# A transformer block with a mixture of experts: head weights split in the keys' loop, experts' down weights split on GpSimd, down as six fp32r products, result stored by tiles

## The reference, cut to what matters

```python
# experts: 2048 tokens, 8 of 64 experts each, rows sorted by expert
gu = lax.ragged_dot(xs, jnp.swapaxes(gate_up_proj, 1, 2), group_sizes)   # 512 -> 2 x 192
gate, up = jnp.split(gu, 2, axis=-1)
hact = jax.nn.silu(gate) * up
y = lax.ragged_dot(hact, jnp.swapaxes(down_proj, 1, 2), group_sizes)     # 192 -> 512
out = jnp.zeros_like(x).at[tok].add(y * w[:, None])
...
# cross attention: 16 heads of 128
q = (hidden_states @ Wq).reshape(B, Sq, H, D)
k = (encoder_hidden_states @ Wk).reshape(B, Skv, H, D)
k = rmsnorm(k, gk)
...
return out @ Wo
```

## Time and profile before

| what | us |
|---|---|
| median of 3 runs (2829.97 to 2833.83) | 2832.93 |
| the profiled execution | 2839.08 |
| its span, first to last instruction | 2837.6 |
| TensorE busy | 2485.7 |
| VectorE busy | 1863.6 |
| ScalarE busy | 1280.9 |
| GpSimd busy | 1542.7 |

### The profile page before, as it was taken

How to read it: one execution, slowest core, us unless ns; L and a number is a source line. 1 busy time by engine, 2 the same in 40 slices (tenths; PEclk the granted TensorE clock), 3 DMA queues, 4 the chain that set the end, 5 groups by cost and what they waited for, 6 DMA issues and landing times. The chain is left out here.

```text
span 2837.6 us, 42365 instructions
## 1 busy us (share of the span) xinstructions
PE 2485.7 (88%) x11365; PEld 1766.0 (62%) x11366; DVE 1863.6 (66%) x3083; ACT 1280.9 (45%) x2516; POOL 1542.7 (54%) x1262
## 2 busy tenths in 40 slices
PE   6898987679793899999999937999999999999797
PEld 2333432267572677777777725778778777877553
DVE  6999999868462346654444456776775776565596
ACT  4566664343562333321222204555555555555385
POOL 2656565432555667676666545655664764444122
PEclk8999999979896899999999967999999999999899
DMA  6989898735675999987777654543444443332101
GB/s 201 289 271 296 267 295 270 218 138 197 237 271 198 334 339 315 342 287 257 265 264 247 204 170 141 180 140 125 158 138 135 159 156 112 123 115 90 60 1 60
DMA packets 271500, 572.10 MB, mean 202 GB/s; under 512 B 26993, under 2 KB 92657, under 8 KB 270593
## 3 DMA queue, kind: packets, MB, share of 16 engines
q1 hardware_dynamic: 218080, 381.54, 40.8%
q0 software_dynamic: 44032, 167.80, 17.6%
q10 hardware_dynamic: 9248, 21.11, 2.2%
HBM read 361.69 MB, written 208.67 MB: 201 GB/s over the span
## 5 line engine op out<-in xcount | busy, mean ns | idle before, releaser
L625 POOL TENSOR_TENSOR b_u<-du,bc 128x1024 f32<-128x1024 f32 x128 | 301.0, 2352 | 214.6 <-DVE c_state L699 111.7
L451 PE MATMUL ps_y<-c_state,ident 128*128 128x512 f32 x512 | 253.6, 622 | 89.0 <-DVE c_state L699 89.0
L2004 ACT ACTIVATE prob<-ps_s,neg,q_rs 128x512 f32<-128x512 f32 x256 | 197.0, 774 | 265.0 <-DVE neg L2194 265.0
L690 DVE TENSOR_TENSOR_SCAN state<-ps_decay,b_u 128x1024 f32<-128x1024 f32 x128 | 292.7, 2287 | 14.6 <-POOL b_u L625 2.3
L1521 PE MATMUL ps_o<-w_dn,hid_t 96*128 x632 | 297.5, 593 | 0.0
L1557 ACT ACTIVATE silu_g<-ps_gu 128x192 f32<-128x192 f32 x159 | 52.5, 330 | 530.1 <-PE ps_gu L1502 530.1
L2098 POOL TENSOR_SCALAR prob<-prob,rden 128x512 f32<-128x512 f32 x256 | 174.7, 692 | 199.9 <-DVE rden L2202 199.9
L451 PEld LDWEIGHTS ps_y<-c_state,ident 128*128 128x128 f32 x512 | 92.9, 194 | 233.6 <-DVE c_state L699 143.8
L1502 PE MATMUL ps_gu<-w_gu_high,rows_t_high 128*128 (+1 forms) x636 | 228.4, 359 | 9.7 <-POOL w_gu_low L1387 8.0
L1387 POOL TENSOR_TENSOR w_gu_low<-raw_gu,w_gu_high 128x1536 fp32r<-128x1536 f32 x64 | 223.8, 3497 | 11.7 <-POOL w_gu_high L1385 11.7
L523 ACT ACTIVATE ps_decay<-delta,a_neg 128x511 f32<-128x511 f32 x256 | 165.6, 681 | 142.2 <-DVE state L690 141.2
(11 more groups left out here) (349 smaller groups left out, 6051.8 us busy)
## 6 DMA issues: line engine op xcount, KB each, us to landing
bc<-bc_dram SPq DMA_DIRECT2D x128, 512.0 KB
raw_gu<-in_gate_up POOLq DMA_DIRECT2D x64, 768.0 KB, 6.0
rows<-rows_dram SPq DMA_DIRECT2D x160, 256.0 KB, 4.8
y_dram<-y SPq DMA_DIRECT2D x158, 256.0 KB, 4.4
rows_dram<-zeros SPq DMA_DIRECT2D x46, 768.0 KB
w_q<-wq_dram SPq DMA_DIRECT2D x64, 512.0 KB, 3.7
w_o<-wo_dram SPq DMA_DIRECT2D x16, 2048.0 KB, 9.6
w_dn<-in_down POOLq DMA_DIRECT2D x64, 384.0 KB, 6.4
```

The lines of the kernel that those rows point to most:

```text
L451: mm = pe.matmul(ps_y[e][:, :], c.ident[:, :], c_state[:, q % 2, g, :], start=False, stop=False)
L625: pool.tensor_tensor(out=b_u[:, q % 2, :, :], in0=slot(du, n).rearrange("p (a l) -> p a l", a=1).broadcast_to([P, G, SEQ]), in1=bc[:, g % ...
L690: dve.tensor_tensor_scan(state[:, q % 2, :], decay[q % 2][:, :], b_u[:, q % 2, :, :].rearrange("p g l -> p (g l)"), 0.0, ALU.mult, ALU.add ...
L2004: act.activation(prob[:, qt, :], ps_s[qt % 2][:, :], ACT.Exp, scale=q_rs[:, k % 2, qt:qt + 1], bias=neg[:, qt:qt + 1], accum_out=den[:, qt ...
```

## The change

The head weights' split moves from GpSimd in the experts' stage to the keys' loop of the dispatch stage. SP loads a pair of heads at the start of each group of 4 tiles and stores split pairs at tiles 8 and 12 and at the end of a pass; ScalarE makes the high part at the start of the next step, VectorE the low part at the end of its group. In the experts' stage GpSimd splits the down weights too, down becomes six fp32r products, and the turned hidden rows are split by ScalarE (high) and VectorE (low). The store of the last ternary chunk moves behind ScalarE's loop. The result is stored by tiles from the feed-forward.

```diff
+        raw_w = p.sb("raw_aw", [P, 2, 2, DM])
+        out_w = p.sb("out_aw", [P, 2, 2, 2, DM], F32R)
+        def pair_no(hg, r):
+            return hg * ST + r
...
-        def rolled(eng, first, second):
+        def rolled(eng, first, second, also=None):
             with eng.Fori(0, ST) as hg:
                 for g in range(NG4 + 1):
+                    if also and g >= 1:
+                        also(hg, g - 1)
                     if g < NG4:
...
+            for i in range(2):
+                sp.sem_inc(aw_stored[i], 32)
+            def load_heads(hg, r):
+                sp.wait_ge(aw_low, pair_no(hg, r) + 1)
+                for h in range(2):
+                    head, to = hg * ST + r % 2 * 2 + h, raw_w[:, r % 2, h, :]
+                    if r < 2:
+                        ins = sp.dma_start(to.rearrange("p (k n) -> p k n", k=KD),
+                                           d["w_q"][bass.ds(head, 1), :, :].rearrange("a p (k n) -> (a p) k n", k=KD))
+                    else:
+                        ins = sp.dma_start(to, d["w_o"][bass.ds(head * HD, HD), :])
+                    ins.then_inc(aw_loaded[r % 2], 16)
+            def store_heads(hg, r):
+                sp.wait_ge(aw_low, pair_no(hg, r) + 3)
+                for h in range(2):
...
+                    sp.dma_start(to, words(out_w[:, r % 2, h, :, :].rearrange("p x n -> p (x n)")))\
+                        .then_inc(aw_stored[r % 2], 16)
             with sp.Fori(0, ST) as hg:
                 for n in range(NT):
+                    if n % G4 == 0:
+                        load_heads(hg, n // G4)
+                    if n in (8, 12):
+                        store_heads(hg, (n - 8) // G4)
                     sp.wait_ge(k_kept, hg * NT + n + 1 + KB)
                     sp.dma_start(m.k_dram[n // ST, n % ST, ds1(hg), :, :].rearrange("a p l -> (a p) l"),
                                  k_out[:, n % G4, :]).then_inc(k_stored[n % G4], 16)
+                store_heads(hg, 2)
+                store_heads(hg, 3)
...
+            for i in range(2):
+                sp.wait_ge(aw_stored[i], 32 * ST * 2 + 32)
...
+            def heads_high(hg, r):
+                act.wait_ge(aw_loaded[r % 2], hg * 64 + r // 2 * 32 + 32)
+                act.wait_ge(aw_stored[r % 2], hg * 64 + r // 2 * 32 + 32)
+                act.activation(out_w[:, r % 2, :, 0, :], raw_w[:, r % 2, :, :], ACT.Copy).then_inc(aw_high, 1)
...
-            rolled(act, square, keep)
+            rolled(act, square, keep, heads_high)
...
+            dve.sem_inc(aw_low, 2)
+            def heads_low(hg, r):
+                dve.wait_ge(aw_high, pair_no(hg, r) + 1)
+                dve.tensor_tensor(out=out_w[:, r % 2, :, 1, :], in0=raw_w[:, r % 2, :, :], in1=out_w[:, r % 2, :, 0, :],
+                                  op=ALU.subtract).then_inc(aw_low, 1)
...
+                    heads_low(hg, g)
...
             def expert(e4, slot, first=False, last=False):
...
-                load_down(e, slot)
...
+                pool_waits(pool, c, dn_loaded[slot], e4 * 16 + 16)
+                pool.tensor_copy(flat(w_dn[0]), raw_dn[:, slot, :]).then_inc(dn_high, 1)
                 if not last:
                     pool_waits(pool, c, gu_ready, e + 1)
                     load_raw(e + WS, slot)
-                pool.wait_ge(dn_loaded[slot], e4 * 16 + 16).then_inc(dn_ready, 1)
...
+                pool_waits(pool, c, dn_high, e + 1)
+                pool.tensor_tensor(out=flat(w_dn[1]), in0=raw_dn[:, slot, :], in1=flat(w_dn[0]),
+                                   op=ALU.subtract).then_inc(dn_ready, 1)
+                if not last:
+                    pool_waits(pool, c, dn_ready, e + 1)
+                    load_down(e + WS, slot)
...
                 for k in range(2):
-                    mm = pe.matmul(ps_o[par][:, :], hid_t[par][:, k, :],
-                                   w_dn[:, ds1(slot), k, :].rearrange("p a f -> p (a f)"),
-                                   start=k == 0, stop=k == 1)
+                    for x, w in ((0, 0), (0, 1), (1, 0)):
+                        mm = pe.matmul(ps_o[par][:, :], hid_t[par][x][:, k, :],
+                                       w_dn[w][:, ds1(slot), k, :].rearrange("p a f -> p (a f)"),
+                                       start=n == 0, stop=n == 5)
+                        n += 1
...
+            def high_hidden(i, par):
+                act.wait_ge(hid_turned, i + 3)
+                act.wait_ge(out_made, i + 1)
+                act.activation(hid_t[par][0][:, :, :].rearrange("p k l -> p (k l)"), ps_h[par][:, :],
+                               ACT.Copy).then_inc(hid_t_high, 1)
...
+        @block.sync
+        def _(sp):
+            for t in range(NT):
+                sp.wait_ge(y_added, t + 1)
+                sp.dma_start(out[t * P:(t + 1) * P, :], c.X[:, t, :]).then_inc(stored, 16)
+            sp.wait_ge(stored, 16 * NT)
...
-        store_output(nc, c, out)
```

More of the change, by code:

```diff
@@ L1314, in experts @@
         hid = [p.sb(f"hid{i}", [P, FI]) for i in range(2)]
-        hid_t = [p.sb(f"hid_t{i}", [FI // 2, 2, P]) for i in range(2)]
+        hid_t = [(p.sb(f"hid_t_high{i}", [FI // 2, 2, P], F32R), p.sb(f"hid_t_low{i}", [FI // 2, 2, P], F32R))
+                 for i in range(2)]
         y = [p.sb(f"y{i}", [P, DM]) for i in range(2)]
@@ L1326, in experts @@
         ended = p.sem("ended")
-        raw_w = p.sb("raw_aw", [P, 2, DM])
-        out_w = p.sb("out_aw", [P, 2, 2, DM], F32R)
-        aw_loaded, aw_high, aw_low, aw_stored = (p.sem(x) for x in ("aw_loaded", "aw_high", "aw_low", "aw_stored"))
         CH, RS, AHEAD = 1024, 4, NE // 2 - 1
@@ L1405, in split_heads @@
-            def split_heads(kind, j, n, following):
-                pool_waits(pool, c, aw_loaded, n * 32 + 32)
-                if not (isinstance(n, int) and n == 0):
-                    pool_waits(pool, c, aw_stored, n * 32)
-                pool.tensor_copy(out_w[:, :, 0, :], raw_w[:, :, :]).then_inc(aw_high, 1)
-                pool_waits(pool, c, aw_high, n + 1)
-                pool.tensor_tensor(out=out_w[:, :, 1, :], in0=raw_w[:, :, :], in1=out_w[:, :, 0, :],
-                                   op=ALU.subtract).then_inc(aw_low, 1)
-                pool_waits(pool, c, aw_low, n + 1)
-                if following:
-                    load_heads(*following)
-                for h in range(2):
-                    to = (m.wq_dram[bass.ds(j * 2 + h, 1), :, :, :, :].rearrange("a p x k n -> (a p) (x k n)")
-                          if kind == "w_q" else
-                          m.wo_dram[bass.ds(j * 2 + h, 1), :, :, :].rearrange("a p x n -> (a p) (x n)"))
-                    pool.dma_start(to, words(out_w[:, h, :, :].rearrange("p x n -> p (x n)"))).then_inc(aw_stored, 16)
@@ L1427, in _ @@
             for slot in range(WS):
                 expert(0, slot, first=True)
-            split_heads("w_q", 0, 0, ("w_q", 1))
-            with pool.Fori(1, J - 1) as e4:
+            with pool.Fori(1, NE // WS - 1) as e4:
                 for slot in range(WS):
                     expert(e4, slot)
-                split_heads("w_q", e4, e4, ("w_q", e4 + 1))
             for slot in range(WS):
-                expert(J - 1, slot)
-            split_heads("w_q", J - 1, J - 1, ("w_o", 0))
-            with pool.Fori(J, 2 * J - 1) as e4:
-                for slot in range(WS):
-                    expert(e4, slot)
-                split_heads("w_o", e4 - J, e4, ("w_o", e4 - J + 1))
@@ L1441, in _ @@
-            for slot in range(WS):
-                expert(2 * J - 1, slot, last=True)
-            split_heads("w_o", J - 1, 2 * J - 1, None)
-            pool.wait_ge(aw_stored, 32 * 2 * J)
+                expert(NE // WS - 1, slot, last=True)
         @block.sync
@@ L1622, in _ @@
                 both(j, True)
-            store_ff(2 * NC - 1)
             with act.Fori(AHEAD, np) as j:
                 both(j, False)
+            high_hidden(np * 2, 0)
+            store_ff(2 * NC - 1)
             for i in range(2):
@@ L2356, in _, with feed_forward @@
                 add(NPP - 1, 1, t, last_banks[t])
-def feed_forward(nc, c, m):
+def feed_forward(nc, c, m, out):
     with ExitStack() as ctx:
@@ L2627, in program @@
             norm_statistics(nc, c, "n3", loads, first=(BATCH - 1) * ST)
-            feed_forward(nc, c, m)
-        store_output(nc, c, out)
-def store_output(nc, c, out):
-    stored = nc.alloc_semaphore("stored")
-    with nc.Block() as block:
-        @block.sync
-        def _(sp):
-            sp.dma_start(out.rearrange("(t p) n -> p t n", p=P), c.X[:, :, :]).then_inc(stored, 16)
-            sp.wait_ge(stored, 16)
+            feed_forward(nc, c, m, out)
 def kernel(x, ctx_1024, L0_xattn_in_proj_w, L0_xattn_conv_w, L0_xattn_conv_b, L0_xattn_x_proj_w,
```

44 lines of the change are left out of this document (23 added, 21 removed).

## The result

The changed kernel takes **2889.34 us** (median of 4 runs, 2887.01 to 2893.23) where the kernel before takes 2833.38 beside it (4 runs, 2829.97 to 2841.97): ratio **1.0194, 95% interval 1.0169 to 1.022**, slower by 56 us. The forecast was 2909, range 2863 to 2953.

The account below looks back on a forecast made before the run. The prediction took the sends to end dispatch and TensorE to bound the experts' stage. 72 + 14 - 10 = +76 us on the profiled 2839.1 gave 2915, or 2909 us in terms of the median, range 2863 to 2953.

Parts of the forecast that it names:

- 72 + 14 - 10: Whole kernel: dispatch 72 us later, experts' stage 14 us longer, end 10 us shorter; sum +76 us.
- the experts' term: Experts' stage: 751 us against 735, taken as +14 us, bounds 0 and +30.
- the 126: Keys' loop: ScalarE's head copies wait for loads and stores, 102 us plus 24 for slower transfers beside the sends.
- the stretch: Keys' loop: beside the sends a transfer takes about 1.4 times as long, adding 24 us of waits.
- they cost 5 to 30 us in their own row: Dispatch: the sends, with more traffic but longer time, slow by 5 to 30 us and stay behind the loop.
- the loop hides it: Rival in dispatch: slack swallows ScalarE's waits, sends end the stage 7 us later; total +11, 2844 us; chance 0.08.
- GpSimd becomes the bound: Experts' stage: GpSimd needs 11.6 us an expert where TensorE needs 10.4, so GpSimd sets the stage's time.
- The end: Program's end: only the last 256 KB follow the last add; -10 us, between -8 and -11.
- Clock: Rival in the keys' loop: TensorE's clock falls to 1.2 GHz, loop ends some 15 us later; 2924 us; chance 0.10.
- What would show it: Signs listed for dispatch, experts and end, including TensorE waiting 60 to 100 us for weights and GpSimd's period 11 to 12.

Follow-up runs that it names:

- early heads: The changed kernel with head weights' loads issued two groups ahead and each pair stored right behind its low part: 2874.22 us, ratio 1.0138.
- the exchanged order: The kernel before with the result stored by tiles and hidden rows turned and split ahead of the next tile's gate and up, down still fp32: 2836.04 us, ratio 1.0005.

## Why the prediction came true, and where it did not

The time lies in the stated range, 20 us under the forecast of 2909. In the profiled executions the terms are 72 + 14 - 10 against 69.7 + 0.0 - 10.2, and 4.1 us of start and 1.3 of the rest come off, which belong to nothing in the change. Most of the miss is the experts' term, which did not come at all. That dispatch came within 2.3 us is in part luck.

**Dispatch.** The mechanism is the forecast one: the copy waits for a transfer that has only just been asked for. Waits 134 against 126 us, copies 16.9 against 17, ScalarE's other waits saved 39 against 45, loop +104.6 against +98, end at 977 against 975 (from a start 4 us earlier). The last stores came as 7.7 us against 8.

The prediction took the landing of the last send, 911 us, for the end of the stage before. It lands at 910.7, but then GpSimd stands in a DRAIN before the next stage can start at 920.1. In the changed kernel it does so beside the loop, where nobody waits for it. The DRAIN before and now (duration in ns, start in us):

```profile
L1133 POOLq DRAIN  x1: 8391/8391/8391, 910.9 to 910.9; - x1
```

```profile
L1133 POOLq DRAIN  x1: 8388/8388/8388, 960.9 to 960.9; - x1
```

So, each counted from its own start, the stage's work ends 78 us later (984.7 against 910.7), but the next stage only 69.7, since 8.4 us of DRAIN are now covered. The loop's growth, 6.6 us more than forecast, and this cover, which the prediction did not have, nearly cancel.

One price inside the 126 was off: the first pair of a later pass was given 6 us, 8.7 with the stretch, and waits 9.9 to 10.1; it is no shorter than the pairs that wait for stores (7.1 to 10.4, mean 9.5). The formula of the Trainium skill's "Anatomy of one DMA" that the prediction sets beside the row is given there for DMAs issued from GpSimd, while SP issues these loads; the sum does not use it.

**The step that failed here: "they cost 5 to 30 us in their own row".** The sends, first to last, took 274.9 us instead of 223.3: +52. It did not show, since the loop ended later still. The early heads show it: the rival "the loop hides it" priced dispatch at +7 with the waits gone, and it came to +55. The argument was that more traffic had more time; the row to look at was the DMA share, 0.70 beside the loop: at 385 GB/s 24 MB are 62 us, and the share leaves 0.30 of 142 us, some 43 us, so they do not fit beside the loop.

**Experts. The step that failed: "GpSimd becomes the bound", with 11.6 us an expert and a tile of 4.1 to 4.3.** Two sizes were off. GpSimd takes 10.95: the waits and table ahead of an expert are 0.46 and 0.75 us in the rows above, not 1.1, and the gap of 0.1 behind the cast of the down weights is not there. And the tile stays at 4.48. The prediction had the chain (low part ready at 1304.42, TensorE at 1304.35) and took it as a loss of at most 0.15 us of the 0.39. It compared the next start with the old time of the low part; but the chain starts with the turned rows, which come behind gate and up, so it runs through each tile and sets the period itself. 2.47 x 4.48 = 11.1 us is just over GpSimd's 10.95, so GpSimd seldom decides (TensorE waits for it 10.3 us in all), though it hardly waits itself. Seven executions with fp32 down have 739.9 to 743.9 us here (leaving the exchanged order out), three with six products in the changed order 737.3 to 740.3: if the six are worth anything, it is about 2 us.

**The end.** -10 forecast, 10.2 measured; 3.1 us are left, under the 4.

**Clock.** Beside the sends the granted clock of the loop fell to 0.81 from 0.95 (means between its two levels, 1.2 and 2.4 GHz; TensorE stood for up to 12 us at a time), and TensorE's 640 instructions take 142.3 us instead of 126.1. The part of the rival that says the clock falls is true, and "HAM oscillation" of the Trainium skill's TensorE: Matmul & The Clock Gate agrees with it. Its price did not come: ScalarE waits only 5.4 us for others in the loop, so 16 us of slower products lie in TensorE's idle time.

**What would show it.** Right: waits of 5 to 10 us, pairs 2 and 3 for the stores, loop in 220 to 260, no sends alone, dispatch's end at 985.7 (992 forecast), under 4 us behind the last add. Wrong: GpSimd's period, PE's waits for the weights (10 us, not 60 to 100) and the tile.

**A version that beats both** is the kernel before with the result stored by tiles: 0.9933 and 0.9956 of it. It is the one part of the change that gains; the heads in the keys' loop lose, and the split of the down weights is worth 0 to 2 us as it stands. The moved store of the last ternary chunk was not run by itself.

## What to carry to other kernels

Before moving traffic into a stage, look at its DMA share, not only at which engine waits: 24 MB that cost nothing beside the experts, where the share was 0.83 but nobody waited for it, cost 55 us beside the sends even when ScalarE no longer waited for the heads themselves. Where a loop issues a load and the very next instruction needs it, the wait is paid each time; ask one step earlier. When one engine's work is made shorter, walk the chain of the next input through the other engines for a whole period, and then ask who is next: here six products were worth 38 us, of which the chain of the turned rows hid 8 and GpSimd, once that was gone, 31. And before calling the last work's end the end of a stage, look for what its engine does behind it: GpSimd's DRAIN of 8.4 us counts only where GpSimd is last.

## What the runs showed of the hardware

More indirect DMAs in flight can be much slower. With two, three and four in flight the keys' loop took 144, 266 and 268 us. While GpSimd issued a send each 1.28 us without a pause, ScalarE and VectorE went on in steps of 10 to 17 us, in the group shown above 38 to 69 us after TensorE's recorded turn of the tile, with no releaser in the profile, at a DMA share of 0.54. The Trainium skill, DMA: Bandwidth & Descriptors, section "Queues, rings and completion order", says that each DMA engine takes turns between the queues that have work. By that rule SP's transfers would be slowed and not stopped; here its issues took 0.33 to 0.36 us each, and what came late were TensorE's results or signals, of which the rule says nothing.

GpSimd ends the dispatch stage with a DRAIN of 8.4 us, in the kernel before (8.391) and in the changed one (8.388). With two sends in flight and the sends last, the next stage starts 12.1 us behind the last send (four kernels: before, store by tiles, early heads, rows first with fp32 down); with the loop last the DRAIN is covered.

Two profiled executions of one kernel differ by 8 to 11 us in the first 730 us and by 0.3 us in dispatch. A difference of 10 us between medians of this kernel is not settled by the total alone; by stage it is. Why the start moves stays open.
